# A macaron block with routed experts: first routing, register lists and attention normalisers rearranged

## What is computed

```python
def ffn(x):                                   # 8 experts, top 1
    probs = softmax(x @ router_W + router_b)
    mask = one_hot(argmax(probs), 8)
    h = relu(einsum('bsd,edf->besf', x, W1) + b1)      # 128 -> 512
    y = einsum('besf,efd->besd', h, W2) + b2           # 512 -> 128
    return einsum('bse,besd->bsd', mask * probs, y)
def attn(x):
    q, k, v = (layernorm(x) * g1 + b1) @ (wq, wk, wv)  # 16 heads of 8
    pq, pk = elu(q) + 1, elu(k) + 1
    x = x + (pq @ sum(pk v) / (pq @ sum(pk) + 1e-6)) @ wo
    return x + gelu_table(round((layernorm(x) * g2 + b2) @ w1 / 0.1)) @ w2
x = x + 0.5 * ffn(layernorm(x))
x = x + attn(layernorm(x))
x = x + 0.5 * ffn(layernorm(x))
```

## Time and profile before

| | us |
|---|---|
| median of 3 runs | 219.54 (219.14 to 219.72) |
| the profiled execution | 220.0 |
| its span, first to last instruction | 218.3 |
| TensorE busy | 194.8 (89%) |
| VectorE, ScalarE, GpSimd busy | 119.6, 117.9, 122.8 |

### The profile page before, as it was taken

The page is one execution under the profiler, slowest core; times in us unless marked ns, Lnnn a source line. Parts: engine busy times, 40 slices in busy tenths (PEclk is TensorE's granted clock), DMA queues, the critical chain, the costliest instruction groups (busy, mean ns, idle before and its releaser), DMA issues.

```text
span 218.3 us, 4513 instructions
## 1 busy us (share of the span) xinstructions
PE 194.8 (89%) x1398; PEld 162.6 (75%) x1398; DVE 119.6 (55%) x494; ACT 117.9 (54%) x338; POOL 122.8 (56%) x191
## 2 busy tenths in 40 slices
PE   4998699999999985968977999998889899999992
PEld 2984248999999953856864587697534899989991
DVE  3746802222225537494866746757551677577762
ACT  3393406665555729758688885041300666656670
POOL 4783477765666788649302354458871154445444
PEclk9999999999999999799999999999988999999998
DMA  5999579989893121089992000011116919676610
GB/s 147 314 353 299 175 226 333 312 266 322 229 317 91 48 72 27 26 336 419 417 411 115 0 0 3 15 39 37 45 53 227 384 51 305 211 257 212 216 63 5
DMA packets 29752, 40.26 MB, mean 184 GB/s; under 512 B 4229, under 2 KB 20392, under 8 KB 28704
## 3 DMA queue, kind: packets, MB, share of 16 engines
q1 hardware_dynamic: 22096, 32.79, 42.2%
q0 software_dynamic: 2496, 4.76, 8.4%
q10 hardware_dynamic: 5136, 2.42, 3.9%
HBM read 10.78 MB, written 14.46 MB: 116 GB/s over the span
## 4 chain that ended last, share of the span: by engine, by line
PE 62%; POOL 11%; DVE 8%; DMA 7%; issue 5%; ACT 4%; SPq 1%; DVEq 0%; POOLq 0%; ACTq 0%
PE bank L978 15%; PE bank L995 14%; PE bank L832 7%; PE bank L1105 6%; PE bank L1121 5%; PE bank L879 4%; POOL xnT L588 3%; POOL rstd L525 3%; DMA eqrq<-row_scratch 2%; DMA x<-in_L_attn_x_dram 2%; PE bank L971 2%; DMA out_dram<-ysb,eqrq 2%; PE bank L848 2%; DMA xnT<-slot_scratch,posu 1%; PE bank L1086 1%
## 5 line engine op out<-in xcount | busy, mean ns | idle before, releaser
L675 ACT ACTIVATE hT<-bank,ewc_own 128x128 f32<-128x128 f32 x184 | 52.5, 368 | 53.1 <-PE bank L978 52.3
L978 PE MATMUL bank<-xT,ewc_own 128*128 128x128 f32 x368 | 49.0, 276 | 0.5 <-DVE xT L1326 0.4
L995 PE MATMUL bank<-ew,hT 128*128 x368 | 48.8, 276 | 0.0
L978 PEld LDWEIGHTS bank<-xT,ewc_own 128*128 128x128 f32 x368 | 45.0, 192 | 1.7 <-issue 1.2
L995 PEld LDWEIGHTS bank<-ew,hT 128*128 128x128 f32 x368 | 44.8, 192 | 0.4 <-issue 0.4
L611 POOL DMA_INDIRECT out_dram<-ysb,eqrq x23 | 22.5, 978 | 29.0 <-DVE ysb L1336 28.1
L567 POOL DMA_INDIRECT Xg<-xn_scratch,srcu x23 | 22.0, 957 | 12.4 <-issue 4.9
L832 PE MATMUL bank<-ones_bf 128*128 128x512 bf16 x67 | 23.7, 495 | 4.7 <-POOL ident L458 2.6
L1332 DVE TENSOR_TENSOR ysb<-bank,ewc_own 128x128 f32<-128x128 f32 x23 | 6.7, 291 | 28.5 <-PE bank L995 27.1
L603 POOL DMA_INDIRECT row_scratch<-pay,posu x16 | 15.8, 988 | 10.9 <-DVE posu L1294 7.6
L588 POOL DMA_INDIRECT xnT<-slot_scratch,posu x16 | 15.6, 976 | 5.0 <-issue 3.9
(11 more groups left out here) (225 smaller groups left out, 319.0 us busy)
## 6 DMA issues: line engine op xcount, KB each, us to landing
ewc_own<-ew SPq DMA_DIRECT2D x46, 322.0 KB, 4.1
row_scratch<-xn SPq DMA_DIRECT2D x8, 1024.0 KB, 10.9
ew<-in_L_ffn_W_dram SPq DMA_DIRECT2D x1, 2048.0 KB, 11.3
slot_scratch<-ysb SPq DMA_DIRECT2D x23, 64.0 KB
ew<-in_L_ffn_W_dram SPq DMA_DIRECT2D x5, 256.0 KB, 8.4
eqrq<-row_scratch SPq DMA_DIRECT2D x15, 70.0 KB, 2.2
x<-in_L_attn_x_dram SPq DMA_DIRECT2D x4, 256.0 KB, 4.8
xn_scratch<-xn ACTq DMA_DIRECT2D x4, 256.0 KB, 5.7
```

Source lines behind the costliest of these rows:

```text
L675: last = A(hT[:, t.slot, c * P:(c + 1) * P], up_bank(k, c)[:, c * P:(c + 1) * P], ACT.Relu, scale=0.5 if m else 1.0, bias=ewc[t.ahead][:, ...
L978: last = mm(up_bank(k, c)[:, c * P:(c + 1) * P], ewc[t.ahead][:, c * P:(c + 1) * P], xT[:, t.slot, :], start=True, stop=True)
L995: last = mm(bank[4 + t.parity][:, 0:D], hT[:, t.slot, c * P:(c + 1) * P], ew[:, bass.ds(e[k], 1), W2_AT + c * D:W2_AT + (c + 1) * D].squee ...
```

## The change

**First routing.** A partition now holds four neighbouring tokens of a batch, so that input and normalised rows move with 2 KB per partition; the iotas follow. The router's bias is loaded by SP behind x, and TensorE's first product waits for the router's weights alone. The fillers change: 6 for 2 at the start, one more ahead of each of the four batches of logits, then 4, 2, 2 and 6 for 5, 1, 4 and 8. GpSimd makes part of its selectors ahead of the first statistics; the shifts go to VectorE, one by batch (`first_shift`). Of the normalised rows GpSimd makes batch 2, ScalarE the others, the fourth last.

**Lists.** VectorE clamps the codes to whole numbers (`codei`) and shifts them right by 4 for the experts (`eid`); GpSimd's three operations go. SP loads codes, once in each routing, and works out the expert of a tile with register arithmetic. TensorE loads its list ahead of `sources` instead of behind it. In the second routing SP also loads rows 5 to 7, at tile 3, which ScalarE did.

**Attention.** The normalisers come from Ln and Exp on ScalarE (`guess_rstd`), with one Newton step on VectorE (`finish_rstd`); GpSimd has none of kind "a", and its bring-backs follow each other. ScalarE makes all of h1. The orders of ScalarE and VectorE are written out by batch. Six fillers ahead of attention become two.

**Second routing.** The last normaliser on GpSimd comes behind one scatter of batch 2 instead of two.

```diff
-    x_v = x_d.rearrange("b (t p) d -> p (b t) d", p=P)
+    x_v = x_d.rearrange("b (p j) d -> p b j d", j=GT)
...
+        def expert_of(code):
+
+            return within(within(code - (code >> (TPE_BITS + 3)), NE * TPE - 1) >> TPE_BITS, NE - 1)
...
-            sp.wait_ge(eid_ready, 1)
-            experts = load_list(sp, eid[0:1, 0:NT], NE - 1)
+            sp.wait_ge(whole_ready, 1)
+            codes = load_list(sp, codei[0:1, 0:NT], NE * TPE - 1)
...
-            sp.wait_ge(list_ready, 1)
-            experts = load_list(sp, lists[0:1, 0, :], NE - 1)
+            sp.wait_ge(codes_ready, 1)
+            codes = load_list(sp, lists[0:1, 0:NT], CODES - 1)
             sp.wait_ge(b2_halved, 1)
             for k in range(NT):
                 t = Tile(k)
-                if k == UNROLL:
-                    sp.wait_ge(codes_ready, 1)
-                    codes = load_list(sp, lists[0:1, 1, :], CODES - 1)
+                if k == FIRST:
                     for g in range(NG):
                         sp.wait_ge(scattered[g], 16 * GT)
+                    for n in range(SURE, UNROLL):
+                        load_rows(sp, Tile(n), codes[n])
                 if k >= UNROLL:
                     sp.wait_ge(out_done[t.ahead], 16 * t.round)
                     load_rows(sp, t, codes[k])
                     sp.wait_ge(o_ready, 1 + k - UNROLL)
                 if k >= FIRST:
                     sp.wait_ge(xg_T, NT + max(1, k - LEAD))
-                load_weights(t, experts[k])
+                load_weights(t, expert_of(codes[k]))
             for u in range(UNROLL):
...
+            for t in range(POOL_ROWS * GT, (POOL_ROWS + 1) * GT):
+                last = g.tensor_scalar(xn[:, t, :], x[:, t, :], mv[:, t, 0:1], rstd[:, t, 0:1], ALU.subtract, ALU.mult)
+            last.then_inc(xn_by_pool, 1)
...
-                pool.wait_ge(code_ready, 1)
-                link(g.tensor_scalar(eidf[:, :], code[:, :], 1.0 / TPE, 0.5 / TPE - 0.5, ALU.mult, ALU.add))
-                link(g.tensor_scalar(eidf[:, :], eidf[:, :], MAGIC, MAGIC, ALU.add, ALU.subtract))
-                g.tensor_scalar(eid[:, :], eidf[:, :], NE - 1.0, None, ALU.min).then_inc(eid_ready, 1)
-                pool.wait_ge(xn_stored, 16 * NG)
+                for b in range(NG):
+                    pool.wait_ge(xn_stored[b], 16)
...
-            bring_back(0)
-            bring_back(1)
-            normaliser(LN_AT["a", 0] - 1)
-            bring_back(2)
-            normaliser(LN_AT["a", 1] - 1)
-            bring_back(3, range(GT // 2))
-            normaliser(LN_AT["a", 2] - 1)
-            bring_back(3, range(GT // 2, GT))
-            normaliser(LN_AT["a", 3] - 1)
+            for b in range(B):
+                bring_back(b)
...
+                ahead_of = GT // 2 if b + 1 < B else 1
+                scatter_rows(b - 1, range(ahead_of))
                 normaliser(LN_AT["m1", b] - 1)
-                scatter_rows(b - 1, range(GT // 2, GT))
+                scatter_rows(b - 1, range(ahead_of, GT))
...
+            def guess_rstd(b):
+
+                ts = slice(b * GT, (b + 1) * GT)
+                act.wait_ge(a_var, 2 * (b + 1))
+                A(alog[:, ts, :], avar[:, ts, :], ACT.Ln).then_inc(a_log, 1)
+                act.wait_ge(a_log, b + 1)
+                A(aguess[:, ts, :], alog[:, ts, :], ACT.Exp, scale=-0.5).then_inc(a_guess, 1)
...
+            renormalise(0)
+            renormalise(1)
+            store_xn(0)
+            store_xn(1)
+            renormalise(3)
+            store_xn(3)
+            store_xn(POOL_ROWS)
...
+            normal1(0)
+            guess_rstd(1)
+            norm1(0)
+            normal1(1)
+            take_kv(0)
+            take_q(0)
+            norm1(1)
+            attention_input(0)
+            take_kv(1)
+            take_att(0)
+            guess_rstd(2)
+            take_q(1)
+            normal1(2)
+            attention_input(1)
+            norm1(2)
+            take_kv(2)
+            take_att(1)
+            take_q(2)
+            guess_rstd(3)
+            normal1(3)
+            attention_input(2)
+            norm1(3)
+            take_kv(3)
+            take_att(2)
+            take_q(3)
+            attention_input(3)
+            normal2(0)
+            norm2(0)
+            normal2(1)
+            normal2(2)
+            take_att(3)
...
-            keep_warm(2)
+            keep_warm(6)
...
+                keep_warm(1)
...
-            keep_warm(5)
+            keep_warm(4)
             ranks()
-            keep_warm(1)
+            keep_warm(2)
             tile_list()
-            keep_warm(4)
-            sources()
+            keep_warm(2)
             pe.wait_ge(eid_ready, 1)
             e = load_list(pe, eid[0:1, 0:NT], NE - 1)
-            keep_warm(8)
+            sources()
+            keep_warm(6)
             experts(0, e)
             pe.wait_ge(w_in, 16 * 10)
-            keep_warm(6)
...
+            def first_shift(g):
+
+                ts = slice(g * GT, (g + 1) * GT)
+                dve.wait_ge(rstd_ready, g + 1)
+                v.scalar_tensor_tensor(out=shift[:, ts, 0:1], in0=rstd[:, ts, 0:1], scalar=-1.0, in1=mv[:, ts, 0:1],
+                                       op0=ALU.mult, op1=ALU.mult).then_inc(shift_ready, 1)
...
+                v.tensor_scalar(codei[:, :], code[:, :], NE * TPE - 1.0, None, ALU.min).then_inc(whole_ready, 1)
...
+                dve.wait_ge(whole_ready, 1)
+                v.tensor_scalar(eid[:, :], codei[:, :], TPE_BITS, None, ALU.arith_shift_right).then_inc(eid_ready, 1)
...
+                    if m == 0 and k == 20:
+                        finish_rstd(0)
...
+            def finish_rstd(b):
+
+                ts = slice(b * GT, (b + 1) * GT)
+                dve.wait_ge(a_guess, b + 1)
+                link(v.scalar_tensor_tensor(out=astep[:, :, :], in0=aguess[:, ts, :], scalar=-0.5, in1=aguess[:, ts, :],
+                                            op0=ALU.mult, op1=ALU.mult))
+                link(v.tensor_tensor(out=astep[:, :, :], in0=astep[:, :, :], in1=avar[:, ts, :], op=ALU.mult))
+                link(v.scalar_tensor_tensor(out=rstd[:, ts, :], in0=astep[:, :, :], scalar=1.5, in1=aguess[:, ts, :],
+                                            op0=ALU.add, op1=ALU.mult))
+                v.scalar_tensor_tensor(out=shift[:, ts, :], in0=rstd[:, ts, :], scalar=-1.0,
+                                       in1=bc(mv[:, ts, 0:1], [P, GT, 2]), op0=ALU.mult, op1=ALU.mult).then_inc(a_ready, 1)
...
+            finish_rstd(1)
             phi_k(0)
-            begin(2)
             phi_q(0)
-            for b in range(B):
-                mask_kv(b)
-                if b >= 1:
-                    begin2(b - 1)
-                divide(b)
-                if b + 1 < B:
-                    phi_k(b + 1)
-                if b == 0:
-                    begin(3)
-                if b + 1 == B:
-                    quantise(0, range(3))
-                residual(b)
-                if b + 1 < B:
-                    phi_q(b + 1)
-            begin2(B - 1)
+            mask_kv(0)
+            combine(2)
+            divide(0)
+            first_statistics(2)
+            phi_k(1)
+            finish_rstd(2)
+            residual(0)
+            phi_q(1)
+            mask_kv(1)
+            combine(3)
+            divide(1)
+            first_statistics(3)
+            phi_k(2)
+            residual(1)
+            phi_q(2)
+            finish_rstd(3)
+            mask_kv(2)
+            begin2(0)
+            divide(2)
+            phi_k(3)
+            begin2(1)
+            residual(2)
+            phi_q(3)
+            mask_kv(3)
+            begin2(2)
+            divide(3)
+            quantise(0, range(3))
+            residual(3)
```

More of the change, by code:

```diff
@@ L42 @@
 ROWS_BY_ACT = 4
+POOL_ROWS = 2
 W2_BY_ACT = 3
@@ L213, in macaron_kernel @@
         xn_ready = sem("xn_ready")
-        xn_stored = sem("xn_stored")
+        xn_by_pool = sem("xn_by_pool")
+        xn_stored = [sem(f"xn_stored{g}") for g in range(NG)]
         xnT_ps = sem("xnT_ps")
@@ L305, in picks @@
             return m * len(PICKS[0]) + 1 + [first + n > g for first, n in PICKS[m]].index(True)
-        LN = [(kind, b) for kind in ("m0", "a", "l", "m1") for b in range(B)]
+        LN = [(kind, b) for kind in ("m0", "l", "m1") for b in range(B)]
         LN_AT = {k: i + 1 for i, k in enumerate(LN)}
@@ L325, in load_list, with within @@
                 skip_runtime_bounds_check_because="the engine that makes the table clamps all of it to this range")[1]
+        def within(value, most):
+            return nc.s_assert_within(value, min_val=0, max_val=most, skip_runtime_bounds_check_because=
+                                      "codes are clamped to 0 to 128, and 128 is taken as 127")
+        def expert_of(code):
+            return within(within(code - (code >> (TPE_BITS + 3)), NE * TPE - 1) >> TPE_BITS, NE - 1)
         def load_rows(eng, t, code):
@@ L469, in _, with end_selectors @@
```

(49 more changed lines are left out.)

124 lines of the change are left out of this document (50 added, 74 removed).

## The result

The changed kernel takes 223.3 us (median of 4, 222.3 to 225.2) beside 219.34 for the kernel before: 1.019 times as long, with a 95% interval of 1.012 to 1.027. The forecast was 217.8, within 215.4 to 220.8, so the prediction was wrong in sign and the time lies outside its range. The profiled execution of after took 222.3, its span is 220.6.

The account below looks back on a forecast made before the run. The chain runs through TensorE for 62% of the span, so only its waits and clock count. Terms -1.5, 0, +1.0, +0.4, -1.6 sum to -1.7; 220.0 - 1.7 - 0.46 = 217.8 us, range 215.4 to 220.8.

Parts of the forecast that it names:

- Second routing: Second routing and last stage: normaliser earlier -0.8, one list operation fewer -0.25, SP's second list load gone -0.55; together -1.6 us.
- Rival 4: Second routing: fillers meet the low clock longer and eat its gain, total 219.2 us; chance 0.08.
- Logits at full clock: First stage: added fillers raise TensorE's clock before the logits, so the last choice of experts ends at 16.1, -1.5 us.
- the floor of 15.6: First stage: earliest end of the choices of experts, set by VectorE's chain of statistics, shifts and picks from 6.9 on.
- the 0.3 of links: First stage: 0.3 us counted for links between operations in VectorE's chain up to the choices.
- Codes instead of experts: First routing from T0, the end of the last choice of experts, to the turned tile: about 0, between -0.6 and +0.6.
- the cover of 0.3: First routing: stores of normalised rows land by 24.4, hidden behind the wait for the source list with 0.3 us to spare.
- First tiles at half clock: Start of the first experts: fillers end ahead of the gather, so the first products run at half rate, +1.0 us.
- Attention: Attention stage: earlier numerators given back by the fourth batch, -0.1 us, plus +0.5 for a possible clock fall.
- rival 3: Attention: clock falls ahead of the fourth keys, stretching keys, values and queries by 1.5 to 3; about 219.6 us, chance 0.12.

Follow-up runs that it names:

- e15: The changed kernel with only its second list moved from byte 92 to byte 128: 217.3 us where before has 218.9, 0.991 times before.
- e16: The kernel before with only its second list moved from byte 92 to byte 128: 0.997 times before (0.995 to 1.000).
- e1: The changed kernel with its second list at byte 128 instead of 92, first run: 231.4 to 236.1 us beside 231.1 to 238.7 for before.
- e7: The changed kernel with its second list at byte 128 and five fillers in each of two attention waits: 0.973 times before (0.963 to 0.983).
- e10: The changed kernel with its second list at byte 128, run again: 0.990 times before (0.983 to 0.996).
- e3: The changed kernel with its second list at byte 128, plus extra SP list loads from several bytes, beside a fill and quiet; its total says nothing.
- e5: The changed kernel with its second list at byte 128, a repeat: 233.7 us where before has 235.7.
- e11: The changed kernel, list at byte 128, fillers changed in first stage, ahead of first tile, in attention and second routing: 0.995 times before (0.989 to 1.001).

## Why the prediction was wrong, point by point

**Second routing: the step that failed.** I wrote "the list loses one of its operations: -0.25", and TensorE's load of that list, 2.26 in before and 7.52 after, stands nowhere in the sum; I looked at how many loads there are, not at which list each reads. The rows had it: 2.04 for 23 values, 2.04 for 8 and 6.08 for 23. I read the first two as "the same for 8 as for 23" and the third as a matter of the moment, though the last two read the same list and agree in 0.26 us per value. The change gives that list to TensorE, the one engine whose load is on the path. Cost: 6.61 in that stage instead of -0.25. Where a row stands out three times over its like, its cause belongs to the sum even if the change seems to remove it. Rival 4, the fillers at low clock, was right as a mechanism (12 fillers took 4.50, 1.9 over the 2.6 of full clock), but here it follows from the load; in e15 the half clock lies under the load again and costs nothing. No rival of mine held the load.

The other two terms of this part held: -0.70 measured against -0.8 for the normaliser (the two times I gave for its end differ by 0.69), and -0.93 for the last stage against -0.55; e16, without SP's slow load, gains as much there.

**Logits at full clock: right in kind, mis-sized.** The clock rose at 6.2 as said, logits took 0.95, VectorE was late next. But oh came at 14.44, not 16.1, below what I called the floor of 15.6. The statistics began at 6.62, not 6.9. The two picks took 1.69 and 1.77: my 1.8 and 1.9 were those of before, where an operation of 0.22 took up to 0.36 now and then. Shift and copy took 0.17 instead of 0.4, since on VectorE an independent instruction starts before the printed end of the last (12.50 and 12.57 for two of 0.15 and 0.18), and the 0.3 of links does not exist. The clock did not fall in the logits here; in e1 it fell at 11.6 and oh was at 16.1.

**Codes instead of experts: right in after, optimistic elsewhere.** srcu stands at T0 + 8.29 (8.55), the tile is turned at T0 + 13.2 (12.9), and from T0 to the first expert product it is 14.74 us where before has 14.34. GpSimd's rows took 3.14 for four, not 1.3 to 2. In after they stayed hidden, but the cover of 0.3 does not always hold: in e7, e10 and e15 the first gather waited for the stores of the normalised rows, in e15 until 24.38 instead of 23.64, and there the tile was turned at T0 + 14.3. So e15's -1.68 for the first stage, near the forecast, is a choice 3.2 earlier (-1.5 forecast) and a ladder 1.5 longer (0 forecast).

**First tiles at half clock: right, mis-sized.** +1.0 against +1.34 for the stage in after and +0.83 in e15; the two groups cost 0.98 and 1.1. The clock came back 6 us behind the turn, later than my 3.6 to 5.0.

**Attention.** The rungs were each 3 to 8% shorter than mine (from y(20) to the end of norm1(0) 5.08 for 5.55, numerators to numerators 7.38 for 7.8 and 9.43 for 9.7), and the same overlap is in them: ScalarE's copies of 0.59 follow each other every 0.48. So -1.25 instead of -0.1, and the fourth batch does not give it all back, though it waits for ScalarE as said. (The terms listed from 95.8 on add up to 101.35, not 101.5, another 0.15 of it.) The half clock of rival 3, for which I took +0.5, is what seven of ten profiles have, at 1.6 to 2.0. With it the stage stands at +0.4 to +0.7 over before, near my +0.4, by two errors that cancel.

**The total.** Without the start byte the kernel takes 0.991 times before; the forecast was 217.8 / 219.5 = 0.992. So the rest of the sum held, but by luck in part: the first stage and the attention each come near their forecast in e15 by two errors of opposite sign.

## What to carry to other kernels

Let every list that is loaded into registers begin at a multiple of 16 bytes, and look at which engine's load waits on the path when two lists change places. Check an outlier among like rows before it is taken for chance. TensorE's waits of 1 to 2 us between dense stretches are worth filling where the array is free anyway; that took the fall out of the attention, and gained nothing measurable ahead of the first experts.

## What was not expected of the hardware

A register load of 23 values took 2.03 us from bytes 0, 96, 112 and 128 and 4.89 from 92, 100 and 104, with next to no transfers running, and 6.96 even from byte 0 beside a fill of 8 MB (e3, each once). The clock of TensorE falls at other moments in executions of one kernel (11.6, 14.4, 16.6 and 17.1 in e1, e5, e15 and e10, back at 32.1, 31.5, 33.6 and 34.3), and with the fall and the rise the first product down of the experts comes anywhere from 31.5 to 34.3. The Trainium skill (TensorE: Matmul & The Clock Gate, Why this matters for your kernels) asks for no long idle gaps between bursts of matmuls. The waits of 1.55 us ahead of the fourth keys are shorter than the gaps that it names, and with them left empty the clock fell there in seven profiles of ten, with them filled in none of five (attention at 34.7 to 34.8). What starts a fall behind such a wait in one execution and not in another is open, as is the longer stage of the first experts in e1 to e11.
